# A two-layer gated cross-attention and mixture-of-experts kernel: the second attention rewritten, its keys and values made in the experts' phase, and three shared FFN units put into its last ticks

## The reference, cut to what matters

```
x = x + tanh(g_xattn[0]) * sigmoid_attention(layernorm(x), ctx)         # 16 heads, 64 keys
x = x + tanh(g_ffn[0])   * experts(layernorm(x))                        # 8 experts, top 1
x = x + tanh(g_xattn[1]) * softmax_attention(layernorm(x), ctx, mask)   # 16 heads, 64 keys
x = x + tanh(g_ffn[1])   * (routed(layernorm(x)) + shared(layernorm(x)))  # 2 experts, top 1, + 1 shared
# softmax_attention: k = ctx @ Wk + bk; v = ctx @ Wv + bv; q = x @ Wq + bq
# routed, shared:    relu(x @ w1 + b1) @ w2 + b2, 256 -> 1024 -> 256
```

## Time and profile before

| | us |
|---|---|
| median of 3 runs | 888.3 |
| the profiled execution | 889.87 |
| its span | 888.4 |
| PE / DVE / ACT / POOL busy | 690.4 / 510.1 / 325.8 / 229.6 |
| mean granted TensorE clock | 0.877 |

### The profile page before, as it was taken

One profiled execution on the slowest core, in us unless ns is written; L12 is line 12 of the kernel. 1 busy time (PEld: TensorE's weight loads), 2 busy tenths in 40 slices (PEclk: granted clock), 3 DMA queues, 4 the chain that ended last, 5 costly groups with the idle time before them and its releaser, 6 DMA issues. The chain is left out here.

```text
span 888.4 us, 14959 instructions
## 1 busy us (share of the span) xinstructions
PE 690.4 (78%) x4920; PEld 633.5 (71%) x4921; DVE 510.1 (57%) x1246; ACT 325.8 (37%) x554; POOL 229.6 (26%) x363
## 2 busy tenths in 40 slices
PE   3787850378899998999834468786657799999997
PEld 3456640368899988999833355564557799999997
DVE  5543224166754488445728888874356655565555
ACT  3532401144533355324433354443224233333331
POOL 8443225300010000000021467452027010112500
PEclk9898965598999999999966788887558999999999
DMA  4950005353531045400012000000036101111202
GB/s 154 397 242 1 1 1 221 130 155 97 187 114 34 24 129 168 163 24 24 18 48 71 24 24 1 0 1 1 1 111 216 60 32 41 47 47 45 85 6 89
DMA packets 20930, 71.79 MB, mean 81 GB/s; under 512 B 4097, under 2 KB 8450, under 8 KB 16802
## 3 DMA queue, kind: packets, MB, share of 16 engines
q1 hardware_dynamic: 13730, 49.76, 15.5%
q0 software_dynamic: 7168, 21.63, 8.1%
HBM read 44.65 MB, written 26.74 MB: 80 GB/s over the span
## 5 line engine op out<-in xcount | busy, mean ns | idle before, releaser
L1479 ACT ACTIVATE e_h<-psum,e_be 128x256 f32<-128x256 f32 x144 | 67.8, 475 | 148.5 <-PE psum L51 146.9
L49 PE MATMUL psum<-e_h_hi,e_w_hi 128*128 128x256 f32 x384 | 110.3, 287 | 6.2 <-DVE e_w_lo L1547 5.5
L50 PE MATMUL psum<-e_h_lo,e_w_hi 128*128 128x256 f32 x384 | 107.9, 281 | 0.0
L51 PE MATMUL psum<-e_h_hi,e_w_lo 128*128 128x256 f32 x384 | 107.8, 281 | 0.0
L1753 ACT ACTIVATE f_h<-psum,f_b 128x256 f32<-128x256 f32 x136 | 63.9, 475 | 118.4 <-PE psum L51 118.2
L1539 DVE CAST e_h_hi<-e_h 128x256 fp32r<-128x256 f32 x144 | 43.5, 302 | 88.9 <-ACT e_h L1479 88.9
L49 PE MATMUL psum<-f_w_hi,f_h_hi 128*128 128x256 f32 x272 | 80.6, 296 | 8.8 <-DVE f_h_lo L1806 8.5
L49 PEld LDWEIGHTS psum<-e_h_hi,e_w_hi 128*128 128x128 f32 x384 | 72.3, 188 | 9.6 <-DVE e_w_lo L1547 8.8
L51 PE MATMUL psum<-f_w_hi,f_h_lo 128*128 128x256 f32 x272 | 78.1, 287 | 0.0
L50 PE MATMUL psum<-f_w_lo,f_h_hi 128*128 128x256 f32 x272 | 78.0, 287 | 0.0
L51 PEld LDWEIGHTS psum<-e_h_hi,e_w_lo 128*128 128x128 f32 x384 | 72.4, 189 | 0.0
(11 more groups left out here) (340 smaller groups left out, 1966.3 us busy)
## 6 DMA issues: line engine op xcount, KB each, us to landing
e_w_raw<-in_W SPq DMA_DIRECT2D x18, 1024.0 KB, 5.7
xs<-zeros SPq DMA_DIRECT2D x6, 1024.0 KB, 9.5
ys<-zeros SPq DMA_DIRECT2D x6, 1024.0 KB, 14.4
w_raw<-in_fw SPq DMA_DIRECT2D x12, 512.0 KB, 4.2
ys<-e_yo POOLq DMA_DIRECT2D x14, 256.0 KB, 2.8
e_xg<-xs POOLq DMA_DIRECT2D x13, 256.0 KB, 3.1
e_w_raw<-in_W SPq DMA_DIRECT2D x6, 512.0 KB, 8.0
ys<-x_norm POOLq DMA_DIRECT2D x10, 256.0 KB, 2.5
```

What stands on the lines that cost most here:

```text
L49: nc.tensor.matmul(out, wh, xh, start=start, stop=False)
L50: nc.tensor.matmul(out, wh, xl, start=False, stop=False)
L51: return nc.tensor.matmul(out, wl, xh, start=False, stop=stop)
L1479: nc.scalar.activation(h32[:, m % RING], ps[:, HIDDEN_BANKS[m % RING], 0:SLOT], ACT.Gelu, bias=be[:, m:m + 1]).then_inc(gelu_ok, 1)
```

## The change: what it does, and the diff

1. Keys and values of the second attention (split, projection, spreading by head, biases) move into `experts_phase`, behind its routing on every engine. Its three memsets stand on GpSimd in `prepare`, that is, ahead of the scatter. The second attention's `w_raw` is now loaded in the first.
2. SyncE copies the last FFN's 6 MB of weights from the input into an internal DRAM tensor `k["fw"]` behind the experts' loads, and waits for it.
3. In the second attention the layer norm's statistics and seed stay on VectorE; its 15 further steps go to GpSimd (`normalise`, which the first attention already uses). All gathers of expert rows are issued at the start, into `xn`.
4. The shared network's first layer is loaded and split in the attention's startup, the second layer at tick 16. Three shared units run in the tail: first layers at ticks 16, 19 and 22, second layers at 17, 21 and 23.
5. In the last FFN the 8 routed half-matrices are loaded straight into their `_lo` tiles, four at a time, and split in place while the first two units (now 3 and 4) run. The six later shared units become three: one before the gathered rows are waited for, two behind.

```diff
@@ experts_phase
+            for which in range(2):
+                for f in range(E1 + 1):
+                    sp.dma_start(k["fw"][which, f], io["fw"][which, f]).then_inc(fw_st, 16)
+            sp.wait_ge(fw_st, 16 * 2 * (E1 + 1))
...
+                nc.gpsimd.memset(f32(kz_hi[:]), 0.0).then_inc(kz0, 1)
+                nc.gpsimd.memset(f32(kz_lo[:]), 0.0).then_inc(kz0, 1)
+                nc.gpsimd.memset(vz[:], 0.0).then_inc(vz0, 1)
 
             route.pool(pool, prepare)
...
+            for j in range(QUADS):
+                for a in range(2):
+                    r = slice(2 * HD * j, 2 * HD * (j + 1))
+                    nc.scalar.activation(of_head(kz_hi, j, a), of_rows(j), ACT.Copy, scale=odd[r, a:a + 1]).then_inc(kzh_ok, 1)
@@ softmax_attention, GpSimd
+            gather(0)
+            nc.gpsimd.memset(bo[:], 0.0).then_inc(bo0, 1)
+            gather(1)
+            norm(0, 0)
+            gather(2)
+            norm(1, 0)
+            gather(3)
+            for n in range(NT + 2 * TB):
...
+                if r == 0 and b + 2 < B:
+                    norm(b + 2, 0)
+                if r == 1 and 0 <= b - 2 < B:
+                    norm(b - 2, 1)
@@ ScalarE
+            norm_1(0)
+            for h in range(2):
+                act.wait_ge(f1_ld[h], 16)
+                nc.scalar.activation(sw1_hi(h), f32(sw1_lo(h)), ACT.Copy).then_inc(f1h_ok, 1)
+            transposed_hi(0, t1_done, th1_ok)
+            act.wait_ge(fb_ld, 32)
+            norm_1(1)
             q_hi(0)
...
+                if n in FIRST:
+                    hidden(FIRST[n])
@@ VectorE, in the ticks
+                if n in FIRST:
+                    hidden(FIRST[n])
+                if n - 1 in SECOND:
+                    add_shared(SECOND[n - 1])
@@ TensorE, in the ticks
+    FIRST = {NT: 0, NT + 3: 1, NT + 6: 2}
+    SECOND = {NT + 1: 0, NT + 5: 1, NT + 7: 2}
...
+                if n in FIRST:
+                    first_layer(FIRST[n])
+                if n in SECOND:
+                    second_layer(SECOND[n])
@@ last_ffn_phase
+        DONE = DRAIN_UNITS
+        LOADS = 4
-        HALF = [(f, which, h) for f, which in ((2, 0), (2, 1), (0, 1), (1, 1), (0, 0), (1, 0)) for h in range(2)]
+        HALF = [(f, which, h) for f, which in ((0, 1), (1, 1), (0, 0), (1, 0)) for h in range(2)]
...
+                if n >= LOADS:
+                    sp.wait_ge(w_ld[n % LOADS], 16 * (n // LOADS))
+                sp.dma_start(f32(parts(n)[1]), k["fw"][which, f, :, h * CH:(h + 1) * CH]).then_inc(w_ld[n % LOADS], 16)
...
-            route.dve(dve, lambda step: weights_lo(step))
-            for n in range(2, EARLY):
-                weights_lo(n)
+            route.dve(dve)
             for u in range(PB):
-                hidden(u, lambda m: weights_lo(EARLY + u * MH // 2 + m // 2) if m % 2 else None)
+                hidden(u, lambda m: weights_lo(u * MH // 2 + m // 2) if m % 2 else None)
...
-            with dve.Fori(PB, UNITS - PB) as u:
-                hidden(u + n1)
+            for u in range(DONE + PB, UNITS - PB):
+                hidden(u - DONE + n1)
...
             tiles = (B - 1) * TB // PB
-            dve.wait_ge(y_used, (UNITS - PB + n1) * HALVES + 2)
+            dve.wait_ge(y_used, (UNITS - DONE - PB + n1) * HALVES + 2)
             dve.wait_ge(got, 16 * NT)
```

More of the change, by code:

```diff
@@ L39 @@
 HIDDEN_BANKS = (2, 3, 6, 7)
+DRAIN_UNITS = 3
 def f32(ap):
@@ new lines, in _, with gather, norm @@
+            steps = 0
+            def gather(b):
+                for t in range(b * TB, (b + 1) * TB):
+                    pool.indirect_dma_start(out=k["xn"][:, t, :], out_offset=None, in_=k["ys0"],
+                                            in_offset=bass.IndirectOffsetOnAxis(ap=k["pos0"][:, t:t + 1], axis=0)).then_inc(yg_ok[b], 16)
+            def norm(b, kind):
+                nonlocal steps
+                q = NTH[b, kind]
+                pool.wait_ge(mv_ok, q + 1)
+                last, steps = normalise(nc, pool, ln_mv[:, q], ln_half[:], ln_tmp[:], ln_rstd[:, q], ln_shift[:, q], ln_step, steps)
+                last.then_inc(rs_ok, 1)
@@ L722, in q_hi, with norm_1, transposed_hi @@
+            def norm_1(b):
+                if b:
+                    act.wait_ge(t1_done, b)
+                norm(b, 0, xq, n1_ok)
+            def transposed_hi(b, done, ok):
+                act.wait_ge(done, b + 1)
+                nc.scalar.activation(k["xT_hi"][:, :, b * S:(b + 1) * S], ps[:, 0:2, :], ACT.Copy).then_inc(ok, 1)
             def q_hi(b):
@@ new lines, in _ @@
+            pe.wait_ge(cst_ok, 6)
+            scores(0)
+            input_T(1)
+            for n in range(TICKS):
+                b, r = divmod(n, TB)
+                if r == 2 and 0 <= b - 1 < B:
+                    weighted(b - 1)
+                if 2 <= n < NT + 2:
+                    probs_T(n - 2)
+                if n + 1 < NT:
+                    scores(n + 1)
+                if r == 0:
+                    if b + 1 < B:
+                        q_proj(b + 1)
+                    if 0 <= b - 2 < B:
+                        pe.wait_ge(tl1_ok, min(b + 2, B))
+                        if b >= 3:
+                            pe.wait_ge(tl2_ok, b - 2)
+                        project(b - 2)
+                if r == 1 and 0 <= b - 3 < B:
+                    pe.wait_ge(y_used, min(b - 1, B))
+                    logits(b - 3)
+                if r == 2 and b + 2 < B:
+                    if b >= 2:
+                        pe.wait_ge(y_used, b - 1)
+                    if b >= 3:
+                        pe.wait_ge(lg_ok, b - 2)
+                    input_T(b + 2)
+                if r == 3 and 0 <= b - 2 < B:
+                    pe.wait_ge(tl1_ok, min(b + 3, B))
+                    pe.wait_ge(y_used, b - 1)
+                    if b >= 3:
+                        pe.wait_ge(lg_ok, b - 2)
+                    rows_T(b - 2)
+                if n in FIRST:
+                    first_layer(FIRST[n])
+                if n in SECOND:
+                    second_layer(SECOND[n])
```

1031 lines of the change are left out of this document (408 added, 623 removed).

## The result

The changed kernel takes 892.68 us (median of 19 runs), the kernel before 888.93 beside it (19 runs): ratio 1.0042, 95% interval 1.003 to 1.0054. It is slower by 0.4%, where I forecast 877.4, that is faster by 1.2%. The profiled execution took 894.95 us (span 893.4), 5.1 more than that of before (889.87, span 888.4).

A forecast was written before the change was run, and what follows sets the result against it. TensorE bounds the kernel from the first slot to the end (busy 176.9 of 178.2 us); elsewhere it waits. 3.3 - 3.6 + 20 - 11.3 - 34.4 + 14.1 + 1 = -10.9: 889.87 becomes 879.0, median 877.4 us, range 866 to 892.

The forecast's parts named there:

- Experts (+3.3): Experts' start: three memsets on GpSimd end at 146.1, the scatter was ready at 142.85, so +3.3 us.
- The copy: Weights' 6.3 MB copy inside DRAM during the experts: 18 to 36 us against 84 us of cover, costing nothing.
- Start and ticks: Second attention's startup and ticks together: -3.6 us, bounds +2 and -9.
- the new wait: Attention startup, ScalarE: q_hi(0) stands behind norm_1(1), which waits for GpSimd's second chain; tick 0 1.9 us later.
- The tail (+20): Second attention's tail with three shared units: 72.7 us against 53.3, taken as +20 us.
- the walk: Tail, step by step: TensorE waits 7 us before project(2), 2.6 before logits(1), 2.8 before project(3), 1.3 before logits(2).
- the dense stretch at full clock: Earlier trace, 16.7 of 20 us busy at clock 1.00; the new tail was expected to resemble it.
- rival B: Tail stays at the low clock, each unit costing 23.8 us instead of 11.9, so the kernel is slower; chance 0.12.
- my threshold: Rival B decides from a third of the tail at 1.2 GHz: 16 us against the forecast gain of 10.9.
- The bound of +55: Tail's upper bound, were all of it at 1.2 GHz: +55 us.
- The last FFN's start: Last FFN's start: first slot at 694.9 instead of 706.2, -11.3 us, bounds -4 to -20.
- Later units, stall, clock: Behind the slots: three shared units fewer -34.4 us, stall for the gathers +14.1, lower clock behind the gap +1.

The follow-up runs named there:

- e1: Changed kernel with the three key/value zeroings moved from GpSimd to ScalarE: 0.7% or 6 us less by the ratios.
- e7: Changed kernel with ScalarE's q_hi(0) ahead of the second norm and the transposes' copy ahead of two splits: 0.5%, 4.6 us less than the unaltered changed kernel.
- e10: Changed kernel with the second attention's norm chains on VectorE instead of GpSimd: 889.31 us against 898.80 for the unaltered changed kernel on the same chip.
- e5: Changed kernel with 59 matmuls into an unused bank added in TensorE's tail gaps: 0.8%, 7 us less than the unaltered changed kernel by the ratios.
- e6: Changed kernel with the tail's same steps reordered on TensorE, ScalarE and VectorE: 1.9%, 17 us less than the unaltered changed kernel by the ratios.
- e3: Changed kernel with two shared units in the attention's tail instead of three, the third behind the slots: 0.7% or 6.6 us less by the ratios.

## Why the prediction was wrong

**Experts (+3.3).** The step that failed is "three memsets stand ahead of the scatter, and the scatter was ready at 142.85". It priced GpSimd's queue and took `pos`, VectorE's product, as given. The memsets held up VectorE as well. The queue's part was 3.7 us of the scatter's delay, near my 3.3; VectorE's step added 3.0, and without the memsets the experts are 7.0 us shorter (e1). I weighed the two engines' collisions for the ticks and not here, where they decide. The copy was hidden. Keys and values were not wholly: without the memsets the first slot is still 3.0 us later than before, and the scatter's issues take 20.8 us instead of 19.4.

**Start and ticks (-3.6; measured -4.4 from B).** Right in sum, and the new wait (q_hi behind the second norm) was the right one: e7 takes most of it away. What I did not ask is what the chains are worth on the other side: e10 shows that their move is a loss of 9.5 us for the kernel, 4.9 at the start, 8.8 in the tail, for 3.4 in the ticks. The tail's part is the clock, with the waits as they were.

**The tail (+20).** This is the step that decides. The waits were in the walk, and came out shorter. What failed is "the new tail, 59 of 73 us busy, is more like the former", the dense stretch at full clock. TensorE was busy 73.9 us, not 59; these 14.9 us are the 14.7 that the tail is longer than forecast. The earlier trace rows had a warning in them: the stretch at 0.50 was one directly behind an idle gap, and the walk itself set four gaps ahead of project(2), logits(1), project(3) and logits(2). I judged by the busy share of the tail, and that says nothing of the clock: this tail was busy for 0.83 of its time, more than the 0.81 I had forecast, at 0.79. That the lower clock is what cost the time is shown by the windows at 0.50 and 0.59 and by three kernels with the same work: with the gaps filled the tail is 9.8 us shorter (e5), with work put into them TensorE needs 11.7 us less for the same matmuls (e6), and with the waits unchanged but the clock higher 8.9 less (e10). That the gaps alone bring it is not shown: e5 still has it behind the logits, e10 lacks it behind three equal gaps. It is rival B's mechanism at under a third of its size (14.9 of 48 us): my threshold, 16 against a gain of 10.9, was nearly met, and the experts' 6.4 us did the rest. The bound of +55 for a tail wholly at 1.2 GHz was too small by my own terms: 59 us doubled and 13.7 of waits make 131.7, or +78. The Trainium skill, "TensorE: Matmul & The Clock Gate", "Why this matters for your kernels", warns of idle gaps between bursts of matmuls. The row at 0.59 behind the wait of 3.33 us agrees, and so does the one at 0.50 behind that of 2.78; the row at 1.00 behind 2.79 us in e10 does not show it. I applied it to one gap at the end and not to the four of the tail.

**The last FFN's start (-11.3; -12.8).** Right.

**Later units, stall, clock (-34.4 + 14.1 + 1; -19.0).** Right in sum and in mechanism, gap included. The clock stayed at its lower level longer than the 3.4 us that I took from the earlier trace rows, 10.2 us from the gap's end (865.12 to 875.30 at 0.50), but VectorE's pace hid most of it, as I had argued: the unit took 12.8 us where 12.3 were counted. But three units in one term hid that the third is worth nothing: e3 shows the end bound by the landing of the gathers as long as VectorE waits for them ahead of the last two units, so that two moved units bring all of the 19 us, and the third pays 7.7 in the tail for none.

The range ended at 892: it took in rivals one at a time, not a mis-sized tail and experts together.

## What to carry to other kernels

Walk a changed stage with the clock in it: write down each gap that the walk sets on TensorE, and each string of very small matmuls, and price what follows at both levels, as a range, since a busy share over the stage says nothing of it. Units moved to cover idle time should stand in the gaps (e6), not behind the steps that wait; and each moved unit is priced alone, against what bounds the place that it leaves. Ahead of a memset on GpSimd, look at what VectorE does meanwhile, not only at what GpSimd does next.

## What the runs showed of the hardware

While GpSimd runs a string of memsets, VectorE's tensor_scalar and conversions wait for its end, however small they are and however the string is cut (6.90, 7.98 and 6.02 us for instructions of 0.17), while its reductions and two-input forms are not held up (0.22 and 0.17 us). TensorE's clock behind one and the same wait differs between kernels: behind 2.78 us it was 0.50 in the changed kernel, behind 2.79 us it was 1.00 in e10, and the same 488 matmuls of the tail took 73.9 and 65.0 us. On two of the four chips of the experiments, ScalarE stood still for 13.5 to 21.5 us during the gathers, and the kernel before was 18 us slower, so that the sign of this change depends on the chip: ratio 1.0042 on one kind, 0.9892 on the other.
